# Self-attention scores: two bf16 products per half against four fp32 row groups, with the order of the PE queue changed

## What is computed

```python
q = jnp.einsum('bsc,hcd->bhsd', xn, wq)      # 16 heads, d = 32, s = 1024
k = jnp.einsum('btc,hcd->bhtd', yn, wk)
v = jnp.einsum('btc,hcd->bhtd', yn, wv)
a = jax.nn.softmax(jnp.einsum('bhsd,bhtd->bhst', q, k) * D ** (-0.5), axis=-1)
mask = (jnp.arange(t)[None, :] > jnp.arange(s)[:, None]).astype(a.dtype)
a = a * mask                                  # self-attention only, after the softmax
o = jnp.einsum('bhst,bhtd->bhsd', a, v)
```

## Time and profile before

| | |
|---|---|
| median of 3 runs | 2523.2 us (2522.53 to 2523.38) |
| the profiled execution: its time | 2524.31 us |
| its span in the trace | 2522.6 us |
| PE busy in the span | 2047.2 us (81%) |
| DVE busy | 1367.6 us (54%) |
| ACT busy | 929.6 us (37%) |
| POOL busy | 710.5 us (28%) |
| mean granted TensorE clock | 0.902 of full speed |

### The profile page before, as it was taken

How to read it: one execution, slowest core, us unless ns; L and a number is a source line. 1 busy time by engine, 2 the same in 40 slices (tenths; PEclk the granted TensorE clock), 3 DMA queues, 4 the chain that set the end, 5 groups by cost and what they waited for, 6 DMA issues and landing times. The chain is left out here.

```text
span 2522.6 us, 36317 instructions
## 1 busy us (share of the span) xinstructions
PE 2047.2 (81%) x11904; PEld 1504.7 (60%) x11904; DVE 1367.6 (54%) x3511; ACT 929.6 (37%) x1859; POOL 710.5 (28%) x1199
## 2 busy tenths in 40 slices
PE   5983974467867677999799979969898589999991
PEld 4661863354444454555455558846687378888991
DVE  4871006535745765888688847757636432222332
ACT  4220321112324346888688843232232112222230
POOL 0223011030130125777577751102330230000005
PEclk9995995578979789999999989979999699999995
DMA  2004531000011286333333430110000525555684
GB/s 87 1 1 150 167 104 28 13 13 14 1 19 12 82 216 165 85 85 85 86 65 92 97 108 11 28 36 1 1 13 1 193 104 175 175 175 175 215 287 115
DMA packets 171504, 219.20 MB, mean 87 GB/s; under 512 B 39911, under 2 KB 133540, under 8 KB 165184
## 3 DMA queue, kind: packets, MB, share of 16 engines
q1 hardware_dynamic: 163344, 196.65, 26.7%
q0 software_dynamic: 7264, 20.31, 2.5%
q10 hardware_dynamic: 720, 0.07, 0.0%
HBM read 171.13 MB, written 46.14 MB: 86 GB/s over the span
## 5 line engine op out<-in xcount | busy, mean ns | idle before, releaser
L2390 DVE TENSOR_REDUCE l3s_mx<-banks 128x1 f32<-128x1024 f32 x256 | 313.1, 1223 | 96.7 <-PE banks L2292 93.8
L2292 PE MATMUL banks<-l_stack 128*128 128x512 bf16 x1024 | 268.1, 385 | 44.1 <-ACT xn_tokens L2373 21.0
L1012 PE MATMUL banks<-l3f_xrt,l3f_w 128*128 128x256 f32 (+1 forms) x1536 | 277.9, 342 | 2.7 <-issue 1.5
L1012 PEld LDWEIGHTS banks<-l3f_xrt,l3f_w 128*128 128x128 f32 x1536 | 249.6, 192 | 29.1 <-issue 3.3
L1302 DVE TENSOR_SCALAR l3f_sg<-banks 128x256 f32<-128x256 f32 (+1 forms) x192 | 72.0, 375 | 287.5 <-PE banks L1012 287.5
L2273 POOL TENSOR_TENSOR xn_tokens<-xn_tokens,l3s_sm 128x1024 f32<-128x1024 f32 (+3 forms) x128 | 201.6, 1575 | 50.3 <-DVE l3s_sm L2397 49.2
L222 PE MATMUL banks<-ident,xn_tokens 128*128 128x128 f32 x320 | 64.7, 338 | 166.8 <-DVE xn_tokens L211 148.0
L2292 PEld LDWEIGHTS banks<-l_stack 128*128 128x128 bf16 x1024 | 80.8, 98 | 163.3 <-ACT xn_tokens L2373 52.6
L2373 ACT ACTIVATE xn_tokens<-banks,l3s_mx 128x1024 f32<-128x1024 f32 x128 | 142.7, 1115 | 46.2 <-DVE l3s_mx L2390 45.1
L222 PEld LDWEIGHTS banks<-ident,xn_tokens 128*128 128x128 f32 x320 | 46.6, 172 | 188.4 <-DVE xn_tokens L211 133.0
L2373 ACT ACTIVATE x_features<-banks,l3s_mx 128x1024 f32<-128x1024 f32 x128 | 143.0, 1117 | 27.9 <-DVE l3s_mx L2390 27.6
(11 more groups left out here) (532 smaller groups left out, 3925.4 us busy)
## 6 DMA issues: line engine op xcount, KB each, us to landing
l3f_w<-in_L_ffn_gate_up_w_dram SPq DMA_DIRECT2D x24, 2048.0 KB, 7.6
l3f_w<-in_L_ffn_down_w_dram SPq DMA_DIRECT2D x24, 1024.0 KB, 6.0
l_stack<-l_q_part SPq DMA_DIRECT2D x72, 256.0 KB, 6.0
l_stack<-l_k_part SPq DMA_DIRECT2D x72, 256.0 KB, 11.4
l0f_w<-in_L_ffn_W_dram SPq DMA_DIRECT2D x16, 1024.0 KB, 5.8
l_q_part<-l_stack SPq DMA_DIRECT2D x24, 256.0 KB, 3.0
l_k_part<-l_stack SPq DMA_DIRECT2D x24, 256.0 KB, 3.7
l3f_rows<-l3f_zero SPq DMA_DIRECT2D x13, 384.0 KB, 4.1
```

The costliest lines, as they stand in the source:

```text
L1012: last = nc.tensor.matmul(ps[:, f % 4, h * PAIR:h * PAIR + size], w1_sb[:, p, dc, h * FF + f * P:h * FF + (f + 1) * P], xrt[:, p, dc, 0:si ...
L2292: last = nc.tensor.matmul(ps[:, 2 * (v % 2) + h, :], stack[p][0][s][:, r, si * P:(si + 1) * P], stack[p][1][s][:, r, h * 512:(h + 1) * 512 ...
L2390: nc.vector.tensor_reduce(mx[:, v % RING:v % RING + 1], ps[:, 2 * (v % 2):2 * (v % 2) + 2, :].rearrange("p a n -> p (a n)"), AX_X, ALU.max ...
```

## The change

- **Scores.** Queries and keys stay fp32. `queries` and `keys` hold two heads on four groups of 32 rows: head u of a pair on groups 2u and 2u+1, with the first half of the keys on the one and the second half on the other. `scores(v)` is called for even v only and makes two units: four fp32 matmuls with 32 rows each, into four banks. There are three score buffers (banks 0 to 5) in place of two.
- **Banks.** Transposed bankfuls and outputs share banks 6 and 7. The dictionary `uses` numbers them in the order in which PE makes them; even numbers are stored by ACT (side 0), odd ones by DVE (side 1), outputs too (`store_output`).
- **Order on PE.** A turn is now `turn(v - 5)`, then `scores(v)`, then, every fourth turn, a tile's whole output, which waits for all bankfuls before it to be stored.
- **Loop.** The `Fori` loop is gone; 8 entries stand in a row. An entry is loaded with 9 DMAs in place of 17.
- **Projection.** No split: ACT stores the queries, DVE the keys, SP sends them as fp32 in one DMA each; POOL has nothing to do; the padding entry is gone.
- **Context attention.** `narrow` now holds for width 32 too, so l3a takes the other way; l0a and l2a stay as they are.

```diff
-    narrow = width * 4 <= KEYS
+    narrow = width * 2 <= KEYS
...
-LOADS = 2 * 2 * 4 + 1
+LOADS = 2 * GROUP + 1
...
+    for m in range(GROUP):
+        rows_of, odd, half = slice(m * L3_WIDTH, (m + 1) * L3_WIDTH), m // 2, m % 2
+        q_head, k_head = (src[n].rearrange("(a o d) n -> o d a n", o=2, d=L3_WIDTH)[odd] for src in (q_scratch, k_scratch))
+        sp.dma_start(queries[rows_of, p], q_head).then_inc(loaded[p], 16)
+        sp.dma_start(keys[rows_of, p], k_head[:, :, half * TOK // 2:(half + 1) * TOK // 2]).then_inc(loaded[p], 16)
+    sp.dma_start(values[:, p], v_scratch[n]).then_inc(loaded[p], 16)
...
-                        high(k, 0)
-                        for m in range(1, 2 * BANKS):
-                            high(k, m)
-                            mid(k, m - 1)
-                        mid(k, 2 * BANKS - 1)
+                        for m in range(BANKS):
+                            act.wait_ge(qk_ready, 2 * BANKS * k + m + 1)
+                            nc.scalar.activation(qk[:, k % 2, m, :], ps[:, m, :], ACT.Copy,
+                                                 scale=L3_WIDTH ** -0.5).then_inc(q_stored, 1)
...
+                    for m in range(BANKS, 2 * BANKS):
+                        dve.wait_ge(qk_ready, 2 * BANKS * k + m + 1)
+                        nc.vector.tensor_copy(qk[:, k % 2, m, :], ps[:, m, :]).then_inc(k_stored, 1)
...
-                    for m in range(2 * BANKS):
-                        remainder(k, m)
+                    store_keys(k)
...
+    SCORES = 3
+
+    uses = {}
+    for v in range(ENTRIES * UNITS + OUT):
+        if TURN <= v < ENTRIES * UNITS + TURN:
+            for g, group in enumerate(groups):
+                if group[0] == (v - TURN) % UNITS:
+                    uses["turn", (v - TURN) // UNITS, g] = len(uses)
+        if v >= OUT and (v - OUT) % R == 0:
+            uses["out", (v - OUT) // R] = len(uses)
+
+    def stored_through(side, n):
+
+        return (n + 2 - side) // 2
...
-        with nc.Fori(0, ENTRIES // BODY) as jj:
...
+                def scores(v):
+                    p, si, pair = v // UNITS % 2, tile_of(v), v % R // 2
+                    if v >= SCORES - 1:
+                        pe.wait_ge(exped, v - SCORES + 2)
+                    for u in range(2):
+                        for h in range(2):
+                            lanes = slice((2 * u + h) * W, (2 * u + h + 1) * W)
+                            last = nc.tensor.matmul(ps[:, 2 * ((v + u) % SCORES) + h, :],
+                                                    queries[lanes, p, pair, si * P:(si + 1) * P],
+                                                    keys[lanes, p, pair, :], start=True, stop=True)
+                    last.then_inc(scores_ready, 1)
...
+                        n = uses["turn", e, g]
+                        if n >= 2:
+                            pe.wait_ge(stored[n % 2], stored_through(n % 2, n - 2))
...
+                def output(w):
+                    e, si = w // KC, ORDER[w % KC]
+                    n = uses["out", w]
+                    for side in range(2):
+                        pe.wait_ge(stored[side], stored_through(side, n - 1))
+                    for c in range(si, KC):
+                        for r in range(R):
...
+                for v in range(ENTRIES * UNITS + OUT):
+                    if TURN <= v < ENTRIES * UNITS + TURN:
+                        turn(v - TURN)
...
+                    if v < ENTRIES * UNITS and v % 2 == 0:
+                        scores(v)
+                    if v >= OUT and (v - OUT) % R == 0:
+                        output((v - OUT) // R)
...
+            def store_output(eng, op, v, side):
+
+                if v < OUT or (v - OUT) % R != 0:
+                    return
+                w = (v - OUT) // R
+                e, si = w // KC, ORDER[w % KC]
+                if uses["out", w] % 2 != side:
+                    return
+                eng.wait_ge(out_ready, w + 1)
...
+            @block.scalar
+            def _(act):
+                for v in range(ENTRIES * UNITS + OUT + 1):
+                    store_output(act, nc.scalar, v - 1, 0)
+                    if v >= STORE:
+                        store_turned(act, nc.scalar, v - STORE, 0)
...
+            @block.vector
+            def _(dve):
+                for v in range(ENTRIES * UNITS + OUT + 1):
+                    store_output(dve, nc.vector, v - 1, 1)
+                    if v < ENTRIES * UNITS:
+                        dve.wait_ge(scores_ready, v // 2 + 1)
```

More of the change, by code:

```diff
@@ L2050, in stage_self_project @@
         yt = sb("yt", [P, DC, T])
[L2052 to L2055 removed]
+        qk = sb("qk", [P, 2, 2 * BANKS, 512])
         vs = sb("vs", [P, 2, 2, HD])
@@ new lines, in turn @@
+                        last.then_inc(turned, 1)
+                def output(w):
+                    e, si = w // KC, ORDER[w % KC]
+                    n = uses["out", w]
+                    for side in range(2):
+                        pe.wait_ge(stored[side], stored_through(side, n - 1))
+                    for c in range(si, KC):
+                        for r in range(R):
+                            last = nc.tensor.matmul(ps[r * W:(r + 1) * W, 6 + n % 2, 0:P],
+                                                    values[:, e % 2, c, r * W:(r + 1) * W],
+                                                    pt[:, w % 2, r, c - si, :], start=(c == si),
+                                                    stop=(c == KC - 1))
+                    last.then_inc(out_ready, 1)
@@ new lines, in store_turned @@
+            def store_turned(eng, op, v, side):
+                if v >= ENTRIES * UNITS:
+                    return
+                e, w = v // UNITS, v // R
+                for g, (u, c0, size) in enumerate(groups):
+                    if u != v % UNITS or uses["turn", e, g] % 2 != side:
+                        continue
+                    n = BANKFULS * e + g
+                    eng.wait_ge(turned, n + 1)
+                    if w >= 2:
+                        eng.wait_ge(out_ready, w - 1)
+                    dst = pt[:, w % 2, v % R, c0:c0 + size, :].rearrange("p c n -> p (c n)")
+                    src = ps[:, 6 + side, 0:size * P]
+                    if side == 0:
+                        last = op.activation(dst, src, ACT.Copy)
+                    else:
+                        last = op.tensor_copy(dst, src)
+                    last.then_inc(stored[side], 1)
@@ L2404, in self_out_weights @@
+        clear_semaphores()
 def self_out_weights(a):
```

321 lines of the change are left out of this document (103 added, 218 removed).

## The result

| | before | after |
|---|---|---|
| median | 2522.9 us (2519.7 to 2523.4, 4 runs) | 2748.3 us (2745.1 to 2752.9, 4 runs) |
| ratio, 95% interval | | 1.0898 (1.0876 to 1.0919) |
| span of the profiled execution | 2522.6 us | 2743.6 us |
| mean granted clock of TensorE | 0.902 | 0.859 |
| first scores of the self-attention | 967.0 | 937.3 |

The forecast was 2616 with a range to 2735. The direction was right; the loss is 225 us where 93 were forecast. By stages it divides so: the projection ends 29.7 us earlier, the self-attention takes 768 us in place of 510 (+258), the context attention l3a is 4.3 us shorter. The three make +224; the spans of the two profiled executions differ by 221, as what lies between and behind these stages is 3 us shorter.

What follows compares the result with a forecast made beforehand. PE was taken as nearly full, with the exp's loop limiting units of few chunks. From 2524.3, self-attention +128, projection -24 and context attention -12 gave 2616 us; own range 2585 to 2650, stated range 2580 to 2735 with 0.78.

Steps and rivals of the forecast that it cites:

- the mechanism and its chain: Self-attention: next maxima wait for maximum, DVE copy, transposes, then scores; 4.96 us a pair, stage 638 against 510.
- A: Self-attention pair whose wide turn's transposes wait for a DVE copy behind the maximum; 5.19 us at 8 chunks.
- B: Next pair: a narrow tile's output waits for a DVE store, and DVE stores it ahead of a maximum; 6.69 us.
- C: Self-attention pair with a narrow turn needing no late bank; the exp's loop as before, 3.6 us.
- D: Self-attention pair where the wide tile's output waits for a DVE copy and the transposes need its bank; 5.15 us.
- rival 2: Self-attention: PE's clock falls to 1.2 GHz, adding 1.7 us a pair, 209 us, total 2825; chance 0.10.
- rival 1: Score matmuls: row groups run two at a time, total 2724, chance 0.12; one after the other 2942, chance 0.03.
- four row groups run four at a time: Self-attention scores: four row groups taken as four times, so 1.05 us for two units; bounds 1.03 and 3.60.
- the prediction's 44 us: Self-attention: cost if each of 2 x 128 tiling-mode changes drained the array for 0.17 us; not in the sum.
- what the maximum waits for: Sign in the self-attention: DVE's maximum waits for PE's scores about 1.5 to 2 us once a pair.
- forecast -24: Projection: shorter pairs, fewer last sends and a removed wait save 24 us, from -30 to -14.
- the term of -0.87 a tile: l3a's loop: smaller output matmuls save 0.87 us a tile while PE is the bound, -11 on about 13 tiles.

Runs made afterwards that it cites:

- last filler run: Changed kernel plus some 1250 useless PE transposes into a free score buffer, ahead of outputs and of turns with v % 4 == 2: 2649.3 us, ratio 1.0499.
- the shorter output wait: Changed kernel with each output waiting only for its own tile's last bankful and its own bank: 2691.1 us, ratio 1.0667.
- scores first: Changed kernel with one edit, on PE scores(v) stands ahead of turn(v-5) again: 2540.6 us, ratio 1.0070.

## Why the prediction missed its range

**Right: the mechanism and its chain.** PE's queue holds the scores back behind transposes that wait for a copy that stands behind a maximum. The kinds of pairs came as forecast, and at full clock nearly with their lengths, in us, for tiles of 8, 7, 6 and 5 chunks:

| kind | forecast | last filler run (clock 0.98) | after |
|---|---|---|---|
| A | 5.19, 5.08, 4.84, 4.73 | 5.37, 5.25, 5.01, 4.90 | 5.36, 5.25, 5.22, 4.90 |
| B | 6.69, 5.82, 5.90, 5.86 | 6.98, 6.08, 6.16, 6.14 | 6.97, 6.08, 7.22, 7.34 |
| C | 3.6 | 3.73 | 3.73 |
| D | 5.15, 5.18, 5.22, 5.25 | 5.49, 5.46, 5.49, 5.51 | 7.65, 6.87, 6.91, 7.00 |
| an entry | 79.3 | 82.7 | 91.7 or 99.4 |

The column of after is an entry of the faster sort; after alternates between the two.

**Wrong: the weight of rival 2.** The sum prices every matmul of the stage at full clock; its term for a falling clock is nothing. Measured, the clock's mean was 0.79 and its price about 100 us. The step that failed is the sentence of rival 2 that took the longest pause, 2.1 us, against a window with 2.67 busy of 5 where the clock stayed at 1.00, and so gave a falling clock a chance of 0.10 and left it out of the range. The pauses were close to the forecast (up to 2.4 us) and the clock fell in a stretch with 3.10 busy of 6. The earlier trace rows was one window, not a bound: the same share of busy time stood there beside a clock of 1.00 and here beside a fall. Nor was it all or nothing: the rival's 209 us were for a stage wholly at 1.2 GHz, and the measured cost is about 100, at a mean of 0.79. A forecast of a stage with such a pause in nearly every pair should have carried a part of the 209 us in its sum, and the whole of it in its range. The miss is also larger than the 13 us by which 2748 lies outside 2735: the range went that far only to cover rival 1, which didn't come, and the forecast's own range ended at 2650.

The Trainium skill ("TensorE: Matmul & The Clock Gate", "A second HAM failure mode: psum-queue depth-cycling") describes another kernel, in bf16, in which short pauses between groups of matmuls make the clock swing between its levels. This trace agrees (1.00 to 0.50 at 1082.2, back at 1085.6, and down again at 1092.5), and the prediction didn't use that section.

**Mis-sized: the terms of a pair.** An entry at full clock is 82.7 instead of 79.3, 27 us over 8 entries. From the copy's end to the transposes it was 0.15 (1068.25 + 0.68 to 1069.08), not the 0.05 taken from other hand-overs; the scores of a pair stand 1.21 us ahead of the maximum (1069.96 to 1071.17), not 1.10. In A the two add 0.21, and A is 0.17 to 0.18 longer; in C only the second stands, and C is 0.13 longer. B and D have more hand-overs and are 0.26 to 0.34 longer; which of them took that stays open. The prediction also let the first five pairs go without transposes where only three do (TURN is five units), some 3 us too few. Sum of the stage: 638 forecast, + 27 for the terms, + 100 for the clock gives 765; measured 768.

**Right: four row groups run four at a time.** Eight records take 1.14 (1.05 forecast, bounds 1.03 and 3.60), so rival 1 falls. Against 3.60 for the same number of records on the full array that is 3.2 times, near the 3.07 of the Trainium skill ("TensorE: Matmul & The Clock Gate", "Measured speedup vs the span model"). Taken on the whole 3.60 the page's ratio gives an estimate of 1.17; the prediction, which took it on 3.44 and added 0.17, had 1.29. No drain shows: the scores start at 1069.96, 0.07 before the transposes' end (1069.08 + 0.95), though the ends of matmuls are modelled in the trace. The change of tiling mode that the Trainium skill ("TensorEngine Tiling (Array Packing)", Key Properties) lets drain the array cost nothing that these rows show: of the 0.17 a change that the prediction's 44 us stand for, at most the 0.09 between 1.14 and 1.05 could be one.

**Right: what the maximum waits for.** The maximum waited for scores 1.9 us a pair (239 / 128), within the 1.5 to 2 forecast.

**Projection: -29.7, forecast -24** (bounds -30 and -14). A pair takes 12.2 us (the norm's transposes at 874.72 and 886.94), as forecast. SP's last send and the first scores of after, against 961.08 in the earlier trace rows and 967.00 in the earlier trace rows:

```profile
933.03 0.91 SPq L2064 DMA_DIRECT2D l_values<-l3p_vs  x2
...
937.25 2.09 PE L2263 MATMUL banks<-l_keys_in,l_queries_in 32*128 32x512 f32 x8 [4.88 <-PEq L44]
```

**Context attention: -4.3, forecast -12** (bounds -20 and +5). The 8.2 us of the earlier trace rows are a tile with a norm's transposes in it; before's next tile has none and takes 7.76, from 1749.65 to

```profile
1757.41 1.04 PE L509 MATMUL banks<-ident,l3a_ex 128*128 128x128 f32 x8
```

In after a tile without a norm takes 7.25, and one with a norm 9.20 (1998.18 to 2007.38):

```profile
1990.93 1.04 PE L509 MATMUL banks<-ident,l3a_ex 128*128 128x128 f32 x8
...
1998.18 1.04 PE L509 MATMUL banks<-ident,l3a_ex 128*128 128x128 f32 x8
...
2003.45 0.66 PE L222 MATMUL banks<-ident,xn_tokens 128*128 128x128 f32 x4 [1.28 <-ACT l3a_heads L708]
```

So the term of -0.87 a tile is mis-sized. Tiles without a norm gain 0.51, as the outputs take 2.86 in place of 3.46 where 2.59 was forecast. Tiles with a norm lose 1.0, as PE stands idle for 1.28 us ahead of the norm's transposes, by the trace for ACT's store of `l3a_heads`, a step that the other way doesn't have. No run was made that takes this wait away.

## What to carry to other kernels

When an order on one engine's queue is changed, read the order of the same two steps on the engine that it hands to: here "transposes, scores" on PE with "copy, maximum" on DVE costs 62 us over before, "scores, transposes" with "maximum, copy" 18. The pairing of the change, "transposes, scores" with "maximum, copy", costs 225, and its mirror image, "scores, transposes" with "copy, maximum", 90 even with the shorter output wait. These are whole times; where the clock fell (0.79, 0.87, 0.93 in the stage) its price is in them. Ask which later instruction stands behind a wait that it doesn't need; the output's wait alone was worth 57 us here in the one order and 43 in the other. And where a change puts a pause of PE into nearly every turn of a stage, put a price on its clock in the sum, even when no single pause is long.

## What the runs showed of the hardware

- The granted clock fell to 0.50 in a stage in which PE's pauses, after the first pair or two, were no longer than 2.4 us (over a hundred of them above 1.5). It fell once in a pause (1082.2) and once under running matmuls (1092.5), so no single pause can be named for it. With the last filler the longest pause, again after the first pairs, was 1.4 us and the mean clock 0.98; with scores first it was 1.5 us and 0.97. With the turn ahead of scores in the kernel before the longest was 1.5 us, but for the break between the loop's iterations, and the clock 0.99.
- Useless work on PE made the kernel faster: 2008 transposes brought 56 us, 1250 better placed ones 99 us. In a fresh design this is a probe, not a remedy; the right order brought 208 us without any.
- Useless work in one kind of pause of four moved the low stretches elsewhere and left the mean clock at 0.79.
- Four fp32 matmuls of 32 rows and 512 columns on four row groups took 1.14 us together at full clock and 2.09 at the lower level (first scores, 937.25).
